# Node terms read in place by the matmuls of a graph kernel, instead of through ScalarE's copies

## The chip, the cores and the metric

The kernel runs on one core of a Trainium2 chip. The engines of the core are named as the profile names them: PE is TensorE, the matrix engine (PEld is its loading of weights), DVE is VectorE, ACT is ScalarE, POOL is GpSimd and SP is SyncE, which only starts transfers. PEq, ACTq and so on are the sequencers of the engines: they step through registers, waits and branches and hand the work to the engine behind them.

The metric is the time on the device for one execution, in microseconds (us). Before the change it was 9471.33 us, the median of three runs (9468.83 to 9475.12).

## The reference

The input is a graph: 6250 nodes with 256 features and 200000 edges, sorted by the node they go to (`dst`). Three things are computed: three graph attention layers over the edges, a linear attention over all nodes, and a layer of eight experts with two per node. The change lies in the graph attention, which reads, cut to what matters:

```
def _gat_conv(h, src, dst, W, att_src, att_dst, bias, heads, concat):
    xh = (h @ W).reshape(n, heads, d)
    a_s = (xh * att_src).sum(-1)
    a_d = (xh * att_dst).sum(-1)
    alpha = jax.nn.leaky_relu(a_s[src] + a_d[dst], NEG_SLOPE)
    amax = jax.ops.segment_max(alpha, dst, num_segments=n)
    e = jnp.exp(alpha - amax[dst])
    z = jax.ops.segment_sum(e, dst, num_segments=n)
    alpha = e / (z[dst] + 1e-16)
    out = jax.ops.segment_sum(xh[src] * alpha[:, :, None], dst, num_segments=n)
    ...
for i, (W, a_s, a_d, b, g, be, heads, concat) in enumerate(layers):
    h_new = _layernorm(_gat_conv(h, src, dst, W, a_s, a_d, b, heads, concat), g, be)
    if i > 0:
        h_new = h_new + h
    h = jax.nn.relu(h_new)
```

The term that matters is `a_d[dst]`, four numbers for each node that must reach each of its edges.

## The kernel before

**Tiling.** The nodes lie in 49 blocks of 128. The edges, sorted by `dst`, are cut into slots of 128 edges; two slots make a group, and all edges of a group go to nodes of one block. Ten groups make a window (20 slots), and a layer has 83 windows, so there are 249 windows in all. The function `edge_phase` works through the windows of one layer. Buffers that end in a number are rings of four windows (`RING`).

**What a window needs.** POOL gathers the rows of the source nodes, one indirect transfer for each slot (L1123, 20 of them, into `G`), and may run four windows ahead of the sums that read them. PE spreads the node term `a_d` over the edges of a slot: a matmul (`spread_ad`, L1275, 20 of them, 128x12 in bf16) multiplies the 0/1 matrix `OHT` with the block's term, which is kept as three bf16 parts for each of the four heads (`terms`, 12 numbers for a node, written by DVE once a layer before the edges begin). DVE makes the scores from it (L1455 to L1467), PE turns them (`turn`, L1284), DVE scans them for the greatest of each node (L1476 onward), PE turns that back (`turn_back`, L1292), DVE subtracts (L1543), ACT takes the exponentials (L1150, L1151). DVE weighs the gathered rows (L1563) and makes the one-hot matrices (L1555), PE sums the edges of each group into PSUM (`sums`, L1317), and DVE adds that to `acc`, the accumulator of the node block (L1581). When a node's edges go on in the next window, the old greatest value is replaced: PE spreads the factor (`spread_fade`, L1304), ACT takes its exponential (`fades`, L1160), and DVE's next scan waits for it.

**Order.** Each engine has its own order written out. A step of PE in window w is: sums of groups 0 to 4, `spread_fade(w+1)`, `turn(w+2)`, sums of groups 5 to 8, `spread_ad(w+3)`, the sum of group 9, matmuls of the linear attention that are mixed in, `turn_back(w+2)`. A step of ACT is: `make_index` (w+5), `exponentials(w+1)`, `load_node(w+4)`, `fades(w+1)`, mixed-in work. At the start of a layer ACT does `make_index` four times and `load_node` four times before its first exponential.

**Which block.** The block of each group depends on the data. A number for each window (`words`) holds the block of group 0 in its lowest six bits and then one bit for each further group that says whether the block moves on by one. `blocks_of` (L1014 to L1023) loads this word into a register of the engine that asks (an instruction TENSOR_LOAD) and works the ten block numbers out in registers. Before the change ACT and DVE ask for it: DVE to know which part of `acc` it adds to, ACT for `load_node` (L1137 to L1143), which copies the 128x12 terms of the ten blocks into a `node` buffer, from which PE's matmuls read at fixed addresses. `load_node` waits until the matmuls of the window four earlier are done (`ad_spread`), and PE waits for `load_node` (`node_ready`).

Of the kernel before, what the change touches and what calls it, by code (L numbers as in the profile page):

```python
# [21 lines left out]
P = 128  # L22
# [12 lines left out]
WG = 10  # L35
# [776 lines left out]
def edge_phase(nc, layer, st, io, dr):  # L812
# [13 lines left out]
    with Phase(nc, f"edges{layer}") as ph:  # L826
        G = [ph.sb(f"G{r}", [P, WS, GW]) for r in range(RING)]
        index = [ph.sb(f"index{r}", [P, WS], I32) for r in range(RING)]
        node = [ph.sb(f"node{r}", [P, WG, KEPT], BF16) for r in range(RING)]
        masks = ph.sb("masks", [P, RING, 1 + 3 * P], BF16)  # L830
# [41 lines left out]
        rels_in = ph.sem("rels_in")  # L872
        node_ready = ph.sem("node_ready")
        front_ready = ph.sem("front_ready")
# [254 lines left out]
        def _(a):  # L1129
# [6 lines left out]

            def load_node(i, n):  # L1137
                w = RING * i + n

                wait_past(a, ad_spread, w - RING + 1)  # L1140
                for g, b in enumerate(blocks_of(a, w)):
                    ins = a.activation(node[n][:, g, :], terms[:, bass.ds(b, 1), :, :].rearrange("p a h k -> p (a h k)"), ACT.Copy)  # L1142
                ins.then_inc(node_ready, 1)  # L1143

            def exponentials(i, n):
# [16 lines left out]
            for n in range(RING):  # L1162
                make_index(0, n)
            for n in range(RING):
                load_node(0, n)

            def step(i, n, mix):
                if mix:
                    centres(i, n)
                if exists(i, n, 1 + RING):  # L1170
                    make_index(*later(i, n, 1 + RING))
                if exists(i, n, 1):
                    exponentials(*later(i, n, 1))
                if exists(i, n) and exists(i, n, RING):
                    load_node(i + 1, n)
                if exists(i, n, 1):
                    fades(*later(i, n, 1))
                if mix:
                    mixes(i, n)
# [86 lines left out]
        def _(pe):  # L1266
            def spread_ad(i, n):
                w = RING * i + n
                pe.wait_ge(oht_ready, 2 * w + 2)
                pe.wait_ge(node_ready, w + 1)  # L1270

                wait_past(pe, ad_ready, w)
                wait_past(pe, ran, w)
                for s in range(WS):
                    mm = pe.matmul(ps_ad[:, s * KEPT:(s + 1) * KEPT], OHT[:, s, :], node[n][:, s // 2, :], start=True, stop=True)  # L1275
                mm.then_inc(ad_spread, 1)
# [1359 lines left out]
```

## Time and profile before

| what | value |
|---|---|
| median of three runs | 9471.33 us (9468.83 to 9475.12) |
| time of the profiled execution | 9454.66 us |
| its span | 9453.0 us |
| granted TensorE clock, mean over the span | 0.724 |
| PE busy | 5285.4 us (56%) |
| DVE busy | 5524.3 us (58%) |
| POOL busy | 5206.4 us (55%) |
| ACT busy | 1795.1 us (19%) |
| L1123, gathers of POOL | 4749.2 us, 4980 of them |
| L1317, sums of PE | 3620.3 us, 9960 matmuls |
| L1142, copies of ACT | 495.9 us, 2490 of them |
| L1275, matmuls that spread the node terms | 173.3 us, 4980 of them |

The profile is of one execution. No engine is busy for more than 58% of the span, so the time is made of waits between engines more than of work. A line of a timeline gives the start, the busy time, the engine, the line of the kernel, what it writes and reads, how many alike follow each other, and in brackets the idle time of the engine before it with what ended that wait. "issue" there means that the profile shows nothing that the engine waited for, and "remote" that a semaphore of another engine ended the wait and no single instruction could be named. Line numbers are those of the kernel before; the change takes 10 lines out ahead of the exponentials and 13 ahead of PE's matmuls.

### The profile page before, as it was taken

The page shows a single profiled execution, that of the slowest core. Times are in us where ns is not written, and L with a number is a line of the kernel's source. Part 1 is how long each engine was busy: PE and PEld are TensorE (multiplying, and loading weights), DVE is VectorE, ACT ScalarE, POOL GpSimd, SP SyncE. Part 2 cuts the span into 40 slices and gives each one's busy share as a digit, 9 for nine tenths or more (in the row PEclk, how much of TensorE's full clock was granted, in tenths as well). Part 3 has the DMA queues.
Part 4 walks back from the last instruction along what each step waited for, and adds up shares of the span by engine and source line. Part 5 has one row for each costly group of instructions (what it writes and reads, how often), then busy time and mean ns, then how long its engine had stood idle before and what let it go on. Part 6 is the DMA issues. An engine that isn't in the chain of part 4 may idle for free. (4 is left out here: it accounts for less than half of the span.)

```text
span 9453.0 us, 126480 instructions
## 1 busy us (share of the span) xinstructions
PE 5285.4 (56%) x21872; PEld 3724.2 (39%) x21873; DVE 5524.3 (58%) x14694; ACT 1795.1 (19%) x6145; POOL 5206.4 (55%) x5539
## 2 busy tenths in 40 slices
PE   4256666655556255565655556266656565553397
PEld 2144444433334144444443334144444443333255
DVE  4355655555558366665665558366666665557543
ACT  2011111110103012222210002122222220102333
POOL 3566666666662565656566662566666666661332
PEclk7677777776667577777776676577777777766699
DMA  3444444444442343444343333344444443334333
GB/s 118 113 137 130 138 130 136 136 129 133 131 132 87 105 117 111 119 113 118 114 117 110 108 112 108 106 114 121 120 120 120 122 116 112 111 107 132 113 55 75
DMA packets 540784, 1098.15 MB, mean 116 GB/s; under 512 B 136232, under 2 KB 332639, under 8 KB 540147
## 3 DMA queue, kind: packets, MB, share of 16 engines
q0 software_dynamic: 274368, 731.65, 28.9%
q1 hardware_dynamic: 264803, 361.17, 12.1%
q14 instruction: 400, 3.28, 0.1%
q8 instruction: 61, 1.00, 0.0%
q10 hardware_dynamic: 1152, 1.05, 0.0%
HBM read 953.54 MB, written 148.64 MB: 117 GB/s over the span
## 5 line engine op out<-in xcount | busy, mean ns | idle before, releaser
L1123 POOL DMA_INDIRECT edges_G<-rows,edges_index x4980 | 4749.2, 954 | 3076.4 <-issue 1389.8
L1317 PE MATMUL edges_ps_o<-edges_G,edges_OH 128*128 128x264 f32 x9960 | 3620.3, 517 | 2818.6 <-DVE acc L1581 1740.4
L1317 PEld LDWEIGHTS edges_ps_o<-edges_G,edges_OH 128*128 128x128 f32 x9960 | 2357.1, 253 | 3772.9 <-DVE acc L1581 1852.1
L1581 DVE TENSOR_TENSOR acc<-acc,edges_ps_o 128x264 f32 x2490 | 1056.9, 424 | 1992.7 <-remote 1038.9
L1563 DVE TENSOR_TENSOR edges_G<-edges_G,edges_ps_c 128x1024 f32<-128x1024 f32 x1245 | 1501.5, 1206 | 44.1 <-ACT edges_G L1151 33.3
L1142 ACT ACTIVATE edges_node<-terms 128x12 bf16 x2490 | 495.9, 210 | 2316.7 <-issue 2283.7
L1555 DVE TENSOR_TENSOR edges_OH<-edges_ps_c,relT 128x512 f32<-128x512 f32 x1245 | 847.1, 681 | 30.5 <-issue 19.2
L1150 ACT ACTIVATE edges_ps_c<-edges_diff 128x80 f32<-128x80 f32 x249 | 60.0, 241 | 2402.8 <-DVE edges_diff L1543 2174.5
L2400 POOL DMA_INDIRECT x<-experts_Y,experts_token x105 | 162.1, 1544 | 373.5 <-issue 211.5
L1476 DVE TENSOR_TENSOR_SCAN edges_run<-edges_masks,edges_ps_s 128x128 f32<-128x128 bf16 x249 | 102.9, 413 | 444.0 <-ACT edges_fade L1160 286.9
L1275 PEld LDWEIGHTS edges_ps_s<-edges_node,edges_OHT 128*128 128x128 bf16 x4980 | 181.5, 104 | 296.6 <-issue 248.8
L1275 PE MATMUL edges_ps_s<-edges_node,edges_OHT 128*128 128x12 bf16 x4980 | 173.3, 172 | 219.9 <-issue 123.7
L1449 DVE TENSOR_SCALAR edges_OHT<-edges_rels,lane 128x1280 bf16<-128x1280 bf16 x498 | 258.8, 561 | 0.0
L2423 PE MATMUL experts_psH<-W,experts_xs 128*128 x420 | 209.6, 622 | 43.5 <-issue 43.3
L1543 DVE TENSOR_TENSOR edges_diff<-edges_alpha,edges_ps_s 128x80 f32<-128x80 f32 x249 | 57.2, 230 | 301.4 <-DMA xn<-node_Hn 106.3
L799 PE MATMUL node_psB<-node_Wx,node_hT 128*128 128x264 f32 x588 | 213.8, 500 | 0.0
L1988 POOL DMA_INDIRECT xslot<-final_XH,final_slots x98 | 97.6, 996 | 198.0 <-DVE final_slots L2168 169.9
L2438 PE MATMUL experts_psY<-W,experts_hT 128*128 x840 | 198.8, 379 | 0.9 <-DVE experts_hT L2527 0.9
L583 POOL DMA_DIRECT2D rows<-node_ext x147 | 80.0, 544 | 212.1 <-ACT node_ext L757 172.3
L2520 DVE TENSOR_TENSOR experts_hid<-experts_psH,b 128x512 f32<-128x512 f32 x105 | 72.6, 691 | 210.9 <-PE experts_psH L2423 202.9
L1444 DVE TENSOR_SCALAR edges_front<-edges_ps_c,edges_rels 128x128 f32<-128x128 f32 x249 | 85.3, 343 | 133.2 <-DMA edges_rels<-rel 60.1
L1304 PEld LDWEIGHTS edges_ps_s<-edges_dropped,edges_front 128*128 128x128 f32 x498 | 119.7, 241 | 108.8 <-issue 80.7
(345 smaller groups left out, 6399.7 us busy)
## 6 DMA issues: line engine op xcount, KB each, us to landing
edges_rels<-rel SPq DMA_DIRECT2D x249, 640.0 KB
edges_G<-rows,edges_index POOLq DMA_INDIRECT x4980
xslot<-edges_blank SPq DMA_DIRECT2D x80, 650.0 KB
edges_links<-links SPq DMA_DIRECT2D x1992, 0.1 KB
rows<-node_ext POOLq DMA_DIRECT2D x147, 130.0 KB, 2.4
edges_masks<-lanes SPq DMA_DIRECT2D x996, 15.0 KB
experts_X<-xslot SPq DMA_DIRECT2D x105, 130.0 KB, 2.1
node_rows<-rows SPq DMA_DIRECT2D x98, 130.0 KB, 2.1
```

The lines of the kernel that those rows point to most:

```text
L799: pe.matmul(psB[slot % 2][:, 0:RW + H], hT[:, slot % TILE_RING, k, :], Wx[:, k, :], start=(k == 0), stop=False)
L1123: g.indirect_dma_start(G[n][:, s, 0:RW], None, dr["rows"], bass.IndirectOffsetOnAxis(index[n][:, s:s + 1], 0)).then_inc(gathered[n], 16)
L1142: ins = a.activation(node[n][:, g, :], terms[:, bass.ds(b, 1), :, :].rearrange("p a h k -> p (a h k)"), ACT.Copy)
L1275: mm = pe.matmul(ps_ad[:, s * KEPT:(s + 1) * KEPT], OHT[:, s, :], node[n][:, s // 2, :], start=True, stop=True)
L1317: mm = pe.matmul(ps_o[BANK_OF[g]][:, 0:GW], OH[:, 2 * g + j, :], G[n][:, 2 * g + j, :], start=(j == 0), stop=(j == 1))
L1449: v.tensor_scalar(OHT[:, s, :].rearrange("p s e -> p (s e)"), rels[:, c * WG * P:(c + 1) * WG * P], lane[:, 0:1], None, ALU.is_equal).then ...
L1555: v.tensor_tensor(OH[:, 4 * k:4 * k + 4, :], ps_iota.unsqueeze(1).broadcast_to([P, 4, P]), rel.unsqueeze(2).broadcast_to([P, 4, P]), ALU.i ...
L1563: v.tensor_tensor(g4[:, :, :, 0:D], g4[:, :, :, 0:D], ps_w[:, 4 * k:4 * k + 4, :].unsqueeze(3).broadcast_to([P, 4, H, D]), ALU.mult).then_ ...
L1581: v.tensor_tensor(a, a, ps_o[BANK_OF[g]][:, 0:GW], ALU.add).then_inc(added, 1)
L2400: g.indirect_dma_start(dr["x2"], bass.IndirectOffsetOnAxis(token[:, slot, :], 0), Y[:, slot, :], None, compute_op=ALU.add).then_inc(y_out, 16)
L2423: mm = pe.matmul(psH[slot % 2][:, :], xs[:, slot % 2, k, :], W1[:, bass.ds(e, 1), k, :].rearrange("p a f -> p (a f)"), start=(k == 0), sto ...
L2438: mm = pe.matmul(psY[slot % 2][:, 0:C], hT[:, slot % 2, c * P:(c + 1) * P], W2[:, bass.ds(e, 1), c, :].rearrange("p a o -> p (a o)"), star ...
```

## The change

ACT's `load_node`, its four `node` buffers and the semaphore `node_ready` are gone. `spread_ad` on PE works out the block numbers of the window itself with `blocks_of` and gives the matmul a slice of `terms` whose address comes out of a register. Nothing is computed otherwise. The functions of DVE, POOL and SP are as before.

```diff
--- before.py
+++ after.py
@@ -826,7 +826,6 @@
     with Phase(nc, f"edges{layer}") as ph:
         G = [ph.sb(f"G{r}", [P, WS, GW]) for r in range(RING)]
         index = [ph.sb(f"index{r}", [P, WS], I32) for r in range(RING)]
-        node = [ph.sb(f"node{r}", [P, WG, KEPT], BF16) for r in range(RING)]
         masks = ph.sb("masks", [P, RING, 1 + 3 * P], BF16)
         links = ph.sb("links", [P, RING, 2, WS], BF16)
         rels = ph.sb("rels", [P, WS * P], BF16)
@@ -870,7 +869,6 @@
         gathered = [ph.sem(f"gathered{r}") for r in range(RING)]
         masks_in = [ph.sem(f"masks_in{r}") for r in range(RING)]
         rels_in = ph.sem("rels_in")
-        node_ready = ph.sem("node_ready")
         front_ready = ph.sem("front_ready")
         oht_ready = ph.sem("oht_ready")
         oh_ready = ph.sem("oh_ready")
@@ -1134,14 +1132,6 @@
                 a.activation(index[n][:, :], srcT[:, bass.ds(w * WG, WG), :].rearrange("p g j -> p (g j)"), ACT.Copy
                              ).then_inc(index_ready, 1)
 
-            def load_node(i, n):
-                w = RING * i + n
-
-                wait_past(a, ad_spread, w - RING + 1)
-                for g, b in enumerate(blocks_of(a, w)):
-                    ins = a.activation(node[n][:, g, :], terms[:, bass.ds(b, 1), :, :].rearrange("p a h k -> p (a h k)"), ACT.Copy)
-                ins.then_inc(node_ready, 1)
-
             def exponentials(i, n):
                 w = RING * i + n
                 a.wait_ge(diff_ready, w + 1)
@@ -1161,8 +1151,6 @@
 
             for n in range(RING):
                 make_index(0, n)
-            for n in range(RING):
-                load_node(0, n)
 
             def step(i, n, mix):
                 if mix:
@@ -1171,8 +1159,6 @@
                     make_index(*later(i, n, 1 + RING))
                 if exists(i, n, 1):
                     exponentials(*later(i, n, 1))
-                if exists(i, n) and exists(i, n, RING):
-                    load_node(i + 1, n)
                 if exists(i, n, 1):
                     fades(*later(i, n, 1))
                 if mix:
@@ -1266,13 +1252,14 @@
         def _(pe):
             def spread_ad(i, n):
                 w = RING * i + n
+                blocks = list(blocks_of(pe, w))
                 pe.wait_ge(oht_ready, 2 * w + 2)
-                pe.wait_ge(node_ready, w + 1)
 
                 wait_past(pe, ad_ready, w)
                 wait_past(pe, ran, w)
                 for s in range(WS):
-                    mm = pe.matmul(ps_ad[:, s * KEPT:(s + 1) * KEPT], OHT[:, s, :], node[n][:, s // 2, :], start=True, stop=True)
+                    at = terms[:, bass.ds(blocks[s // 2], 1), :, :].rearrange("p a h k -> p (a h k)")
+                    mm = pe.matmul(ps_ad[:, s * KEPT:(s + 1) * KEPT], OHT[:, s, :], at, start=True, stop=True)
                 mm.then_inc(ad_spread, 1)
 
             def turn(i, n):
```

How PE's order changes is seen in the loop of layer 0, between the last matmuls of group 8 and those of group 9. Before (`edges_ps_s` is the PSUM tile that takes the spread terms, ISA and REGISTER_ALU are steps of the sequencer, L809 and L1312 are waits with a computed count):

```order
L1312 REGISTER_ALU
L809 REGISTER_ALU
L1317 MATMUL edges_ps_o<-edges_G,edges_OH 128x264 x2
L1269 ISA
L1270 REGISTER_ALU
L1275 MATMUL edges_ps_s<-edges_node,edges_OHT 128x12 x20
L809 REGISTER_ALU
L1317 MATMUL edges_ps_o<-edges_G,edges_OH 128x264 x2
```

After, on the same engine at the same place (L1014 is `blocks_of`, L1262 the matmul of before's L1275, L1304 the sums):

```order
L1299 REGISTER_ALU
L809 REGISTER_ALU
L1304 MATMUL edges_ps_o<-edges_G,edges_OH 128x264 x2
L1014 ISA
L1014 TENSOR_LOAD words
L1014 ISA x2
L1256 ISA
L1262 REGISTER_ALU
L1262 ISA
L1262 MATMUL edges_ps_s<-terms,edges_OHT 128x12 x2
L1262 REGISTER_ALU x2
L1262 ISA
```

Ten pairs of matmuls stand there with two REGISTER_ALU and an ISA between each two pairs, and then the same two rows of group 9 as before; the one run of 20 matmuls has become ten pairs behind a load from memory into a register. On ACT, at the same time in the program, this is where the exponentials lead into `load_node` before:

```order
L1150 ACTIVATE edges_ps_c<-edges_diff 128x4x20
L1151 ACTIVATE edges_G<-edges_diff 128x4x20
L1016 TENSOR_LOAD words
L1016 ISA x2
L1142 REGISTER_ALU
L1142 ISA
L1142 ACTIVATE edges_node<-terms 128x12
L1142 REGISTER_ALU x2
L1142 ISA
```

The copies go on to ten, and then comes L1160, the exponential of the fade. After, from `make_index` to the first mixed-in work:

```order
L1132 ACTIVATE edges_index<-srcT 128x20
L1140 ACTIVATE edges_ps_c<-edges_diff 128x4x20
L1141 ACTIVATE edges_G<-edges_diff 128x4x20
L1150 ACTIVATE edges_fade<-edges_ps_s 128x4
L1172 ACTIVATE edges_xs<-edges_ps_r 128x256
```

L1150 is now the exponential of the fade; it follows the two exponentials of the scores at once. ACT's step has lost ten copies and the register steps of its sequencer that led to them (on average 19 ALU_OP, 10 FUSED_REGOPS and one TENSOR_LOAD a window).

## Rows read from the trace of the kernel before

**Rows 1.** The page, busy time, share of the span and instructions of an engine.
```profile
PE 5285.4 (56%) x21872; PEld 3724.2 (39%) x21873; DVE 5524.3 (58%) x14694; ACT 1795.1 (19%) x6145; POOL 5206.4 (55%) x5539
```

**Rows 2.** The page, costliest groups: count, busy, mean ns of one, idle before.
```profile
L1123 POOL DMA_INDIRECT edges_G<-rows,edges_index x4980 | 4749.2, 954 | 3076.4 <-issue 1389.8
```

**Rows 3.** Waits of POOL, ACT, PE, DVE: total us, times, longest.
```profile
POOL edges_G L1123 <- remote: 1212.5, 369, 5.7
...
ACT edges_node L1142 <- issue: 2283.7, 1159, 7.2
...
PE edges_ps_o L1317 <- DVE acc L1581: 1740.4, 586, 13.9
...
DVE acc L1581 <- remote: 1038.9, 296, 9.0
...
DVE edges_run L1476 <- ACT edges_fade L1160: 286.9, 47, 12.1
...
DVE edges_run L1476 <- issue: 99.9, 35, 6.6
```

**Rows 4.** Timeline around 2202 us: start, busy, engine, line, idle before.
```profile
2202.23 0.17 ACT L1160 ACTIVATE edges_fade<-edges_ps_s 128x4 f32<-128x4 f32 x1 [1.89 <-issue]
...
2202.50 0.42 DVE L1476 TENSOR_TENSOR_SCAN edges_run<-edges_masks,edges_ps_s 128x128 f32<-128x128 bf16 x1 [7.25 <-ACT edges_fade L1160]
...
2203.08 0.94 POOL L1123 DMA_INDIRECT edges_G<-rows,edges_index  x1 [3.10 <-remote]
```

**Rows 5.** Timeline, start of layer 0.
```profile
320.43 0.48 PE L1292 MATMUL edges_ps_s<-ident,edges_greatest 128*128 128x128 f32 x1 [1.85 <-issue]
...
350.82 0.24 DVE L1543 TENSOR_TENSOR edges_diff<-edges_alpha,edges_ps_s 128x80 f32<-128x80 f32 x1 [29.99 <-DMA xn<-node_Hn]
...
351.12 0.94 POOL L1123 DMA_INDIRECT edges_G<-rows,edges_index  x1 [0.30 <-issue]
...
366.28 0.21 ACT L1142 ACTIVATE edges_node<-terms 128x12 bf16 x1 [3.34 <-issue]
...
368.52 1.22 DVE L1563 TENSOR_TENSOR edges_G<-edges_G,edges_ps_c 128x1024 f32<-128x1024 f32 x1 [16.38 <-ACT edges_G L1151]
...
382.88 0.94 POOL L1123 DMA_INDIRECT edges_G<-rows,edges_index  x1 [30.82 <-PE edges_ps_o L1317]
```

**Rows 6.** Timeline, start of layer 1.
```profile
3177.72 0.24 DVE L1543 TENSOR_TENSOR edges_diff<-edges_alpha,edges_ps_s 128x80 f32<-128x80 f32 x1 [29.87 <-DMA h<-node_Hn]
...
3195.97 1.22 DVE L1563 TENSOR_TENSOR edges_G<-edges_G,edges_ps_c 128x1024 f32<-128x1024 f32 x1 [16.93 <-ACT edges_G L1151]
...
3210.34 1.01 POOL L1123 DMA_INDIRECT edges_G<-rows,edges_index  x1 [29.96 <-PE edges_ps_o L1317]
```

**Rows 7.** Timeline, start of layer 2.
```profile
6047.28 0.21 ACT L1142 ACTIVATE edges_node<-terms 128x12 bf16 x1 [3.98 <-issue]
...
6055.17 0.24 DVE L1543 TENSOR_TENSOR edges_diff<-edges_alpha,edges_ps_s 128x80 f32<-128x80 f32 x1 [17.47 <-DMA h<-node_Hn]
...
6056.40 1.21 DVE L1563 TENSOR_TENSOR edges_G<-edges_G,edges_ps_c 128x1024 f32<-128x1024 f32 x1
...
6070.73 1.04 POOL L1123 DMA_INDIRECT edges_G<-rows,edges_index  x1 [33.22 <-PE edges_ps_o L1317]
```

**Rows 8.** Sequencer steps by line: count, ns min/median/max, first and last start.
```profile
L1142 ACTq ALU_OP  x4731: 2/38/1683, 252.3 to 8512.4; - x198
...
L1312 PEldq ALU_OP  x768: 32/32/36, 625.1 to 8542.7; - x192
...
L2371 PEldq FUSED_REGOPS  x330: 42/151/168, 8915.1 to 9419.8; - x165
...
L2371 PEldq TENSOR_LOAD <-owner x210: 296/303/632, 8914.5 to 9419.2; - x105
```

**Rows 9.** Timeline, the 20 matmuls of one window at 2017 us.
```profile
2017.81 0.71 PE L1275 MATMUL edges_ps_s<-edges_node,edges_OHT 128*128 128x12 bf16 x20
```

**Rows 10.** Window at the end of layer 0: length, busy PE, PEld, DVE, ACT, POOL.
```profile
2858.00:2875.00 17.00, 12.54 (x46) 8.59 (x44) 15.59 (x38) 0.68 (x3) 0.00 (x0) 0.90 0.00 0
```

## The prediction

> **What bounds the kernel now.** I read the page first: no engine is busy for more than 58% of the span [rows 1], so what counts is who waits for whom. The group of POOL's gathers comes next: 4980 of 0.954 us each with 3076.4 us of idle time before them [rows 2]. The ordinary gap between two gathers is 0.30 us [rows 5], so one costs 0.954 + 0.30 = 1.25 us, a window of 20 costs 25 us, and all 249 windows 6245 us. Of the idle time 4980 x 0.30 = 1494 us is that gap; 1582 us is more than it. Three waits take 30.82 + 29.96 + 33.22 = 94 us of that, one at the start of each layer, where POOL has filled its four windows and waits for the first sums [rows 5 to 7]. The other 1488 us are 6.0 us a window. So a window takes 25 + 6 = 31 us, and POOL's gathers are four fifths of it. A change gains only if it makes those 6 us smaller, or the three waits of 30 us.
>
> Then the waits of each engine, to see what the 6 us are. POOL waited 1212.5 us in 369 waits, 3.3 us each, for sums; PE waited 1740.4 us for DVE's additions; DVE waited 1038.9 us for PE's results [rows 3]. They wait for each other in a ring. A timeline shows how: PE finished turning back a window at 320.43 + 0.48 us, and DVE, which wants just that, started at 350.82, with POOL gathering without a break until 352 [rows 5]. PE's result was 30 us old when DVE saw it. At the end of layer 0, where POOL gathers nothing, DVE is busy 15.59 of 17 us [rows 10]: there the same ring has hardly a wait. So results of PE reach the others late while something else is going on, and gathers are the first suspect. ACT's copies are the second. Their sequencer steps take 38 ns at the median but up to 1683 [rows 8], and the idle time before the copies is 2283.7 us in 1159 waits that nothing in the profile ended [rows 3]: ACT crawls through register steps through much of the span.
>
> **Part by part: ACT at the starts of the layers.** ACT has 40 copies to make before its first exponential. In layer 0 the last of them is at 366.28; the scores were there at 350.82, and DVE waited 16.38 us for the exponential, until 368.52 [rows 5]. Layer 2 shows the same pair with ACT free, from 6055.17 to 6056.40, 1.23 us apart [rows 7]. With no copies, layer 0 gains 368.52 - 350.82 - 1.23 = 16.5 us, and layer 1 3195.97 - 3177.72 - 1.23 = 17.0 us [rows 6]. In layer 2 the copies ended at 6047.28, before the scores, so ACT's order cost nothing; but DVE's wait of 17.47 us ended only 8 us after them, with POOL still since 6070.73 - 33.22 = 6037.5: between 0 and 17.5 us. Sure are 33.5 us, and with half of layer 2 it is 42. The upper bound is all of POOL's three waits, 94 us, if PE's results also come through earlier without ACT's crawl beside them. Between 42 and 94 I take the middle, 68 us. All of it counts in the span, since POOL stands still and the whole layer is shifted. What is late next there is PE's held result, then the 14 us of DVE and PE from the exponential to the first free buffer.
>
> **ACT in the windows.** `load_node` stands ahead of `fades`, and DVE's scan waits for the fade. DVE lost 286.9 us in 47 waits that ended with the fade, and 99.9 us in 35 more before the same scan [rows 3]: 387 us in all, the upper bound for this term; the lower is 0, since a wait for the fade only may cover one that comes anyway. One such place: fade at 2202.23, scan at 2202.50 after 7.25 us, POOL's gather at 2203.08 after 3.10 us [rows 4]. A pause of POOL of that length is no more than its mean, 3.3 us, so what the fade costs the span is at most POOL's pause and not DVE's 7.25. For the 47 waits that is 47 x 3.3 = 155 us. The pause would often be there for another late result, so I take half, 78 us. What is late next is PE's result for DVE's addition, as in the 296 waits for it. The 495.9 us of the copies themselves count nothing beyond this: ACT is the idlest engine. The wait of ACT on `ad_spread` and that of PE on `node_ready` go too; PE's matmuls of window w+3 had `node` filled a window before, so nothing was waiting there but at the layers' starts.
>
> **PE.** Each window adds, ahead of and between the 20 matmuls, the steps that ACT had: 4731 / 249 = 19 ALU_OP [rows 8], ten FUSED_REGOPS and one TENSOR_LOAD. On PE's sequencer an ALU_OP takes 32 ns, a FUSED_REGOPS 151 and a TENSOR_LOAD 303 [rows 8], from the experts' code for the last two: 0.61 + 1.51 + 0.30 = 2.42 us. The 20 matmuls took 0.71 us in a run [rows 9] and would lie inside it, so the step is longer by 1.7 us where nothing hides it. Behind it on PE stand the sum of group 9, the mixed-in matmuls and `turn_back`, and DVE and POOL wait for all three. Bounds: 249 x 1.7 = 426 us lost, and 0. That the block is read in `terms` and not in `node` costs nothing: same partitions, same 12 numbers, address given a register earlier.
>
> The Trainium skill bears on this twice. It says (Advanced Engine Details and Errata, Engine Queue Depths) that TensorE's queue is 64 deep and the others' 8: by that the chain would be hidden whenever 2.4 us of matmuls are queued, and the term nearer 0; no row here shows the depth. And it says (Runtime: NRT & Kernel Launch, Instruction fetch mechanics) that loading a register costs about 200 ns; the row has 303, and by the page the chain would be 0.1 us a window shorter.
>
> **The sum.** -68 - 78 + 50 = -96 us on the profiled execution's own 9454.66 us: 9359 us. That execution is 16.7 us below the median of the runs, so the median to expect is 9471.33 - 96 = 9375 us.
>
> **Rivals.**
> Layer starts only. The gathers' pace takes up what the fades give, because the pause of POOL is ended by a late PE result and not by the fade. For it: 369 waits of POOL against 47 of DVE for the fade. Then the time is 9471 - 68 + 50 = 9453, or 9403 with PE's chain hidden; about 9428.
>
> PE's chain is on the path. The wait ahead of group 8 ends late in most windows, the queued work is short, and group 9 and `turn_back` come 1.7 us later in each. It decides from (68 + 78) / 249 = 0.59 us exposed a window. Fully exposed it costs 426 us, the fades then gain nothing, as PE is the late one, and the layer starts 68: 9471 + 426 - 68 = 9829. At half of it, 0.85 us or 212 us, it is 9615. For it: DVE's 296 waits for PE's results, 3.5 us each. Against: PE is busy for 56% of the span, and its results are held up for microseconds after they are done, which hides a delay of one or two.
>
> ACT's crawl is what holds PE's results. Then the pauses of POOL shrink everywhere. If half of the 6 us a window goes, it is 249 x 3 = 747 us, about 8720. If a quarter goes it is 373 us, 9098. For it: DVE's wait in layer 2 went on for 17.7 us after POOL's last gather had ended, with ACT crawling through ten of them [rows 7]. Against: in the windows the waits end in POOL's pauses, and a gather costs 1.25 us whatever ACT does.
>
> The change doesn't do what it says for the time: crawl and copies were only a sign of POOL's transfers and covered by them, the 33 us at the starts come back as later waits for the held results, and PE's chain costs the rest: 9471 within 19 us.
>
> **How the numbers follow.** The forecast has a chance of 0.34, layer starts only 0.22, of which 0.17 beyond what can be measured, the large gain 0.12: 0.63 for faster. No difference is the other 0.05 and 0.12 for the change that does nothing: 0.17. PE's chain has 0.20. Faster means by over 0.2%, 19 us, about what a measurement of this kernel can tell from no change. The likeliest case's own range is 9280 to 9440 us, from the fades' 155 and the starts' 94 to a smaller gain of each. The range for 8 in 10 runs from 9120, which takes in the fades' 387 us and reaches nearly to a quarter of the large gain, to 9600, where PE's chain is half exposed.
>
> **What would show it.** In the profile after: L1142 gone and DVE's first weighing within 2 us of the scores' difference in all three layers, against 17 now; POOL's three waits below 20 us each instead of 30; DVE's waits for the fade under 100 us. The 20 matmuls of a window spread over less than 2.5 us, with the wait of the additions for PE not longer than now. The forecast is wrong if the three waits of POOL stay near 30 us, if a window still takes 31 us with DVE's waits merely renamed, or if the sum of group 9 follows group 8 by over 2 us in most windows while POOL waits for it.

## The result, and the profile after

The changed kernel takes 9729.69 us (median of four runs, 9694.83 to 9751.17), the kernel before beside it 9473.10 us. The ratio is 1.0268, with a 95% interval of 1.0237 to 1.0299: 257 us slower, where 96 us faster was forecast and 9600 us was the upper end of the range. The profiled execution took 9723.87 us with a span of 9722.2 us. In the fences of the changed kernel, before's L1123 (gathers) is L1121, L1160 (fade) L1150, L1275 (matmuls that spread the node terms) L1262, L1292 (`turn_back`) L1279, L1317 (sums) L1304, L1476 (DVE's scan) L1463, L1543 (difference of the scores) L1530, L1563 (weighing) L1550 and L1581 (addition) L1568; the further runs move some lines again. A register step that takes over 0.3 us is called slow below, and "crawl" is the state in which many steps are slow.

The page of the changed kernel: POOL's busy time and its gathers answer to [rows 1, 2], and beside them stand the matmuls that spread the node terms.

```profile
PE 5283.8 (54%) x21872; PEld 3771.9 (39%) x21873; DVE 5516.7 (57%) x14694; ACT 1314.8 (14%) x3654; POOL 5218.6 (54%) x5539
...
L1121 POOL DMA_INDIRECT edges_G<-rows,edges_index x4980 | 4759.8, 956 | 3337.4 <-issue 1393.5
...
L1262 PE MATMUL edges_ps_s<-terms,edges_OHT 128*128 x4980 | 475.0, 177 | 1989.8 <-issue 1813.0
```

POOL's idle time before the gathers was 3076.4 us [rows 2] and is 3337.4: 261 us more, and the span is 9722.2 - 9453.0 = 269 us longer. Nearly all of the loss is waiting of POOL. The idle time of PE before the 20 matmuls is 1989.8 / 249 = 8.0 us a window.

The waits of the changed kernel, which answer to [rows 3]:

```profile
POOL edges_G L1121 <- PE edges_ps_o L1304: 1172.4, 401, 31.1
POOL edges_G L1121 <- remote: 736.5, 245, 5.4
...
PE edges_ps_s L1262 <- issue: 1813.0, 889, 63.1
PE edges_ps_o L1304 <- DVE acc L1568: 1088.8, 432, 12.1
...
DVE acc L1568 <- remote: 918.7, 253, 9.6
DVE acc L1568 <- PE edges_ps_o L1304: 582.4, 178, 11.9
...
DVE edges_diff L1530 <- PE edges_ps_s L1279: 110.9, 54, 4.7
...
DVE edges_run L1463 <- ACT edges_fade L1150: 78.8, 15, 9.8
```

Two lines of the kernel before stand in no group of rows and belong beside these:

```profile
POOL edges_G L1123 <- PE edges_ps_o L1317: 439.2, 229, 33.2
...
DVE acc L1581 <- PE edges_ps_o L1317: 120.9, 74, 5.1
```

POOL's waits for sums ("remote" and PE together) were 1212.5 + 439.2 = 1651.7 us and are 736.5 + 1172.4 = 1908.9: 257 us more, of the 269 that the span is longer. PE waits less for DVE's additions than before (1088.8 against 1740.4 us), since it now spends that time, and more, ahead of L1262 on "issue". DVE waits for the fade for 78.8 us instead of 286.9, as was forecast, but its wait for PE's sums has grown from 120.9 to 582.4 us. The sequencer steps say what "issue" is (count, ns min/median/max); they answer to [rows 8]:

```profile
L1262 PEldq ALU_OP  x4731: 2/36/1702, 255.3 to 8818.2; - x198
L1262 PEldq FUSED_REGOPS  x2490: 3/53/1606, 255.4 to 8818.3; - x192
...
L1014 PEldq TENSOR_LOAD <-words x249: 296/302/829, 250.8 to 8814.3; - x125
```

The median of an ALU_OP is 36 ns, but the greatest is 1702: what ACT's steps did before, PE's do now. Over all ALU_OP and FUSED_REGOPS of the two traces, 1850 of ACT's 9625 steps were slow before and none of PE's 5068; in the changed kernel none of ACT's 1840 and 1291 of PE's 12682. The slow steps have moved with the chain. The matmuls of one window in the timeline; they answer to [rows 9], which are of another window:

```profile
2215.58 0.15 PEld L1262 LDWEIGHTS edges_ps_s<-terms,edges_OHT 128*128 128x128 bf16 x1
2216.01 1.14 PE L1262 MATMUL edges_ps_s<-terms,edges_OHT 128*128 x12
...
2217.37 0.20 PE L1262 MATMUL edges_ps_s<-terms,edges_OHT 128*128 x2 [0.21 <-issue]
...
2219.01 0.20 PE L1262 MATMUL edges_ps_s<-terms,edges_OHT 128*128 x2 [1.44 <-issue]
...
2220.56 0.54 PE L1262 MATMUL edges_ps_s<-terms,edges_OHT 128*128 x4 [1.36 <-issue]
2220.72 0.43 DVE L1568 TENSOR_TENSOR acc<-acc,edges_ps_o 128x264 f32 x1 [3.58 <-remote]
...
2221.20 2.12 PE L1304 MATMUL edges_ps_o<-edges_G,edges_OH 128*128 128x264 f32 x4
2221.22 1.01 POOL L1121 DMA_INDIRECT edges_G<-rows,edges_index  x1 [2.39 <-remote]
```

The first 12 matmuls follow each other in 1.14 us; then a pair comes only every 1.4 to 1.6 us, and the last four end at 2221.1. What was 0.71 us is 5.5 us from the first weight load on, and the sum of group 9 (2221.20) stands behind it. Over all windows the sum of group 9 starts 8.6 us after that of group 8 has ended, against 1.9 before, and over 2 us after it in 97% of the windows, against 27%: the prediction's own sign of a wrong forecast. DVE's addition and POOL's gather in this fence don't wait for that sum, which ends only at 2223.3: the addition is of group 8, whose sum had ended at 2216.2, 4.5 us earlier. Both kinds of wait are there. In the 144 windows in which POOL stands idle for over 0.8 us ahead of the gathers that need the sum of group 9, it goes on 1.5 us after that sum's end (before: 204 windows, 6.7 us), so there the late sum itself is what it waits for; for the sums of groups 5 and 7 it goes on 8 to 10 us after their end, in both kernels. The start of layer 0, which answers to [rows 5]:

```profile
345.81 0.24 DVE L1530 TENSOR_TENSOR edges_diff<-edges_alpha,edges_ps_s 128x80 f32<-128x80 f32 x1 [31.27 <-DMA xn<-node_Hn]
...
347.04 1.22 DVE L1550 TENSOR_TENSOR edges_G<-edges_G,edges_ps_c 128x1024 f32<-128x1024 f32 x1
...
356.40 1.23 PE L1262 MATMUL edges_ps_s<-terms,edges_OHT 128*128 x8 [8.75 <-issue]
...
359.25 0.20 PE L1262 MATMUL edges_ps_s<-terms,edges_OHT 128*128 x2 [1.61 <-issue]
...
363.26 0.20 PE L1262 MATMUL edges_ps_s<-terms,edges_OHT 128*128 x2 [3.81 <-issue]
...
367.90 0.20 PE L1262 MATMUL edges_ps_s<-terms,edges_OHT 128*128 x2 [4.45 <-issue]
...
369.69 0.87 PE L1262 MATMUL edges_ps_s<-terms,edges_OHT 128*128 x6 [1.59 <-issue]
...
370.47 0.45 PE L1279 MATMUL edges_ps_s<-ident,edges_greatest 128*128 128x128 f32 x1
...
374.92 0.95 POOL L1121 DMA_INDIRECT edges_G<-rows,edges_index  x1 [23.87 <-PE edges_ps_o L1304]
```

DVE weighs 1.23 us after the scores' difference, not 17.7: its wait for ACT is gone. But the ten blocks of the fourth window on PE now take from 356.40 to 370.56, with `turn_back` and the first sums behind them, and POOL's wait is 23.87 us instead of 30.82. The three waits of POOL are 23.9, 24.4 and 31.2 us, 79.4 together against 94.0: 14.6 us are gained there instead of 68.

### The profile page after: what moved, and what is told of

It reads as the page before. It is cut to its first block and busy times, and to the rows that moved or that the text cites. A ratio compares the mean times of both kernels' runs of the same rounds, so it can differ in the third digit from the quotient of the medians.

```text
span 9722.2 us, 123665 instructions
## 1 busy us (share of the span) xinstructions
PE 5283.8 (54%) x21872; PEld 3771.9 (39%) x21873; DVE 5516.7 (57%) x14694; ACT 1314.8 (14%) x3654; POOL 5218.6 (54%) x5539
## 5 line engine op out<-in xcount | busy, mean ns | idle before, releaser
L1121 POOL DMA_INDIRECT edges_G<-rows,edges_index x4980 | 4759.8, 956 | 3337.4 <-issue 1393.5
L1304 PE MATMUL edges_ps_o<-edges_G,edges_OH 128*128 128x264 f32 x9960 | 3287.1, 481 | 1776.1 <-DVE acc L1568 1088.8
L1304 PEld LDWEIGHTS edges_ps_o<-edges_G,edges_OH 128*128 128x128 f32 x9960 | 2206.3, 236 | 2528.5 <-DVE acc L1568 1168.4
L1568 DVE TENSOR_TENSOR acc<-acc,edges_ps_o 128x264 f32 x2490 | 1055.1, 424 | 2221.2 <-remote 918.7
L1262 PE MATMUL edges_ps_s<-terms,edges_OHT 128*128 x4980 | 475.0, 177 | 1989.8 <-issue 1813.0
L1550 DVE TENSOR_TENSOR edges_G<-edges_G,edges_ps_c 128x1024 f32<-128x1024 f32 x1245 | 1501.5, 1206 | 5.3 <-issue 5.3
L1262 PEld LDWEIGHTS edges_ps_s<-terms,edges_OHT 128*128 128x128 bf16 x4980 | 312.5, 106 | 2234.4 <-issue 2217.5
L1530 DVE TENSOR_TENSOR edges_diff<-edges_alpha,edges_ps_s 128x80 f32<-128x80 f32 x249 | 58.2, 234 | 657.9 <-DMA h<-node_Hn 332.8
L1150 ACT ACTIVATE edges_fade<-edges_ps_s 128x4 f32<-128x4 f32 x249 | 43.2, 174 | 1973.1 <-PE edges_ps_s L1271 662.2
L1463 DVE TENSOR_TENSOR_SCAN edges_run<-edges_masks,edges_ps_s 128x128 f32<-128x128 bf16 x249 | 102.1, 410 | 159.2 <-ACT edges_fade L1150 78.8
L1558 DVE TENSOR_TENSOR acc<-acc,edges_fade 128x260 f32 x249 | 107.3, 431 | 120.5 <-issue 104.6
```

The costliest lines, as they stand in the source:

```text
L1121: g.indirect_dma_start(G[n][:, s, 0:RW], None, dr["rows"], bass.IndirectOffsetOnAxis(index[n][:, s:s + 1], 0)).then_inc(gathered[n], 16)
L1304: mm = pe.matmul(ps_o[BANK_OF[g]][:, 0:GW], OH[:, 2 * g + j, :], G[n][:, 2 * g + j, :], start=(j == 0), stop=(j == 1))
L1550: v.tensor_tensor(g4[:, :, :, 0:D], g4[:, :, :, 0:D], ps_w[:, 4 * k:4 * k + 4, :].unsqueeze(3).broadcast_to([P, 4, H, D]), ALU.mult).then_ ...
L1568: v.tensor_tensor(a, a, ps_o[BANK_OF[g]][:, 0:GW], ALU.add).then_inc(added, 1)
```

## The experiments

Chips differ in this case, so each ratio is to the kernel before on the same chip, and the time of that kernel is given with it. Profiles of before are those of the first chip, at 9454.66 us; against them only differences of many per cent of a wait are read. Eighteen further runs were made.

**The chain of steps, or the copies, or the place of reading.** Kernel before 9462.32 us.

e1, PE reads a fixed block:

```diff
-                blocks = list(blocks_of(pe, w))
-                    at = terms[:, bass.ds(blocks[s // 2], 1), :, :]
+                    at = terms[:, 0:1, :, :]
```

> The kernel after, but every matmul that spreads node terms reads block 0 at a fixed address, so neither PE nor ACT works out block numbers in registers; left out is the right block, all else is done. Theory A (PE's register steps crawl beside POOL's gathers and stand ahead of the last sums): well below the kernel before, 9473 less the 68 to 150 us that ACT's copies cost, so 9320 to 9410 us, and PE's idle time before the 20 matmuls falls from 8.0 us a window to under 2. Rival B (what costs is that ACT's copies no longer separate the engines, or that the matmuls read `terms` itself): stays near 9730 us.

Measured: 9409.69 us, ratio 0.9942 (0.9925 to 0.9959), at the upper edge of what theory A expected (L1261 is the spreading matmul here). From the page:

```profile
L1121 POOL DMA_INDIRECT edges_G<-rows,edges_index x4980 | 4760.6, 956 | 3017.1 <-issue 1390.7
...
L1261 PE MATMUL edges_ps_s<-terms,edges_OHT 128*128 128x12 bf16 x4980 | 170.9, 172 | 180.7 <-issue 139.3
```

The idle time before the 20 matmuls is 0.7 us a window. So PE's steps cost the way from 0.9942 to 1.0268, 0.0326 x 9473 = some 310 us (the two intervals together leave 275 to 345). What `load_node` on ACT had cost is 53 us, if reading `terms` in place costs nothing, and nothing speaks against that: a matmul takes 172 ns on average in both kernels. POOL's three waits at the layers' starts are 18.6, 20.2 and 31.1 us here, 24 us less than before: with no chain on ACT or PE at all, the starts give 24 us and not 68.

e2, the changed kernel with `load_node` put back on ACT, its copies unread:

> The kernel after, with ACT's ten copies a window and their register steps put back beside PE's; nobody reads the copies. Theory A, with ACT's chain on the path too, at the starts and before the fades: 9730 plus 70 to 150 us, 9800 to 9880. Rival C (ACT's chain never cost anything, or the engines' crawl is shared, so that two chains make each other slower): 9730 within 20 us if it cost nothing, over 9950 if they slow each other.

Measured: 9841.25 us, ratio 1.0401 (1.0381 to 1.0422), 1.3% or some 125 us above the changed kernel's ratio: within theory A's range. DVE's wait for the fade is back:

```profile
DVE edges_run L1475 <- ACT edges_fade L1158: 257.9, 39, 10.5
```

e3, the kernel before with ACT's copies at fixed addresses:

```diff
-                for g, b in enumerate(blocks_of(a, w)):
-                    ins = a.activation(node[n][:, g, :], terms[:, bass.ds(b, 1), :, :]...
+                for g in range(WG):
+                    ins = a.activation(node[n][:, g, :], terms[:, g:g + 1, :, :]...
```

> The kernel before, but ACT's ten copies read blocks 0 to 9 at fixed addresses: the copies stay, their register steps go; left out are the right blocks. Theory A says that the steps and not the copies cost: 9473 less 70 to 150 us, 9320 to 9400, within 20 us of the kernel with fixed blocks on PE. Rival D (the copies themselves matter, or nothing on ACT does): 9473 within 20 us.

Measured: 9430.97 us, ratio 0.9963 (0.9951 to 0.9976), a gain of 31 us: less than the 70 to 150 of theory A and more than rival D's 20. The copies then stand without a gap:

```profile
L1142 ACT ACTIVATE edges_node<-terms 128x12 bf16<-128x12 bf16 x2490 | 278.4, 198 | 0.0
```

So ACT idled ahead of its copies on their register steps alone, 2316.7 us before and 0.0 here, and those steps were worth 0.4% of the time.

e4, `spread_ad` behind the sum of group 9 instead of ahead of it:

> The kernel after, with the matmuls that spread the node terms moved behind the sum of group 9 on PE; nothing is left out. If what costs is that the last sum of the window (and with it the buffers that POOL waits for, and DVE's last addition) stands behind the crawling steps, the time falls by a third to all of the loss, to 9480 to 9650 us. If it is the results behind them (scores of window w+3, and turn_back), or only the total of PE's sequencer time, it stays at 9730 within 30 us.

Measured: 9889.79 us, ratio 1.0469 (1.0435 to 1.0503). Slower still by 2.0%, which neither expectation had: it is not the sum of group 9 alone that waits. `turn_back` now stands right behind the chain, and DVE's difference of the scores wants its result:

```profile
L1530 DVE TENSOR_TENSOR edges_diff<-edges_alpha,edges_ps_s 128x80 f32<-128x80 f32 x249 | 59.0, 237 | 1445.5 <-PE edges_ps_s L1279 893.1
...
DVE edges_diff L1530 <- PE edges_ps_s L1279: 893.1, 130, 16.5
```

DVE's idle time there is 1445.5 us, from 657.9 in the changed kernel and 301.4 in the kernel before; 893.1 us of it are put down to `turn_back`, from 110.9 in the changed kernel (in its waits above). What stands behind the chain on PE pays for it.

**How long the chain is, and where.** Kernel before 9371.38 us, another chip.

e5, one block number for all 20 matmuls:

```diff
-                blocks = list(blocks_of(pe, w))
+                blocks = [next(blocks_of(pe, w))] * WG
```

> The kernel after, but all 20 matmuls of a window read the block of group 0: one load into a register and one mask instead of ten numbers; left out are the right blocks of groups 1 to 9. Theory A says that what costs is the number of register steps between the matmuls (29 of them, some at 0.7 us beside POOL's gathers): with 3 of them left, close to the kernel with fixed blocks, 9410 to 9450 us. Rival E (the load from memory into a register, or a matmul with an address out of a register, costs most of the 320 us): 9600 or more.

Measured: 9320.40 us, ratio 0.9945 (0.9928 to 0.9961), the same as with no register at all (0.9942). The load into a register and the address out of one cost nothing that is measured here.

e6, five numbers, each for two groups:

```diff
+                blocks = [b for b, _ in zip(blocks_of(pe, w), range(5)) for _ in range(2)]
```

> The kernel after with five block numbers instead of ten, each read by two groups; left out are the right blocks. Theory A, cost in proportion to the steps: 9410 + 320 x 14/29 = 9565 us, between 9520 and 9620. Rival E: above 9680. A third (only a chain long enough to outlast the queued sums costs): below 9480.

Measured: 9341.45 us, ratio 0.9964 (0.9950 to 0.9978). Half the chain costs 0.2%, not the 1.6% of proportion. The time lies where the third theory put it (its 9480 stood for a kernel before of 9462, a ratio of 1.002), but its reason, a chain that outlasts the queued sums, isn't shown by this run: in a chain of 14 steps few are stretched at all, as the table shows.

```profile
L1262 PE MATMUL edges_ps_s<-terms,edges_OHT 128*128 x4980 | 253.4, 173 | 252.1 <-issue 105.6
```

1.0 us of idle time a window, against 8.0 for ten blocks. The table has, of each four steps of a chain, the share that is slow (over 0.3 us), over the 249 windows; the steps are ALU_OP and FUSED_REGOPS at the line of the copies or of the matmuls, 29 a window:

```
share of slow steps       1-4   5-8   9-12  13-16  17-20  21-24  25-28   first to last, mean
before, on ACT            0.02  0.05  0.17  0.31   0.38   0.44   0.34    12.3 us
after, on PE              0.00  0.00  0.08  0.39   0.39   0.25   0.12     9.8 us
e6, on PE (14 steps)      0.00  0.00  0.05  0.25                          2.3 us
e13, on PE, faster chip   0.00  0.00  0.00  0.00   0.00   0.00   0.00     3.2 us
```

(The 29th step, slow in 29, 10 and 0% of the windows, is left out.) A chain on PE starts fast every time and turns slow at about its twelfth step. The place of the step in the chain is one part of it, and how long POOL has gathered is another. Counting a run of gathers as broken by a gap of over 1 us, a step of ACT's chain in the kernel before was slow in 1% of the cases in the first 2 us of a run, in 29% at 5 to 6 us, and in 82 to 83% from 10 to 20 us. In the changed kernel, at 10 to 20 us of a run, none of 636 steps with places 1 to 8 was slow and 229 of 255 with places 17 to 29 were; in the first 2 us of a run, 18 of 258 of the latter.

e7, the chain woven between the sums, four blocks ahead of the sum of group 7, three ahead of 8, three ahead of 9:

> The kernel after with PE's 20 matmuls and their register steps woven between the sums: four blocks ahead of the sum of group 7, three ahead of group 8's, three ahead of group 9's. Nothing is left out. If the place of the chain makes the loss (it stands in one piece where nothing covers it), part of its steps now lies in PE's waits for DVE's additions and the time falls by 50 to 150 us, to 9580 to 9680. If the sequencer's total time makes the loss, it stays at 9730 within 30 us.

Measured: 9417.33 us, ratio 1.0052 (1.0035 to 1.0068). Nothing is left out, and four fifths of the loss are gone: 2.2% or some 200 us, where 50 to 150 were expected.

e8, the kernel before with added pauses in POOL's gathers:

```diff
+                    if k:
+                        for _ in range(2):
+                            g.value_load(words[0:1, 0:1], min_val=0, max_val=64 * 2 ** (WG - 1) - 1)
```

> The kernel before with four added pauses of about 1 us in each window of POOL's gathers (two register loads ahead of chunks 1 to 4, results unused); nothing is left out. Theory F: long unbroken runs of gathers are what slows register steps and holds PE's results; with shorter runs the crawl before ACT's copies falls clearly below 2284 us, and of the 4 us added a window much comes back out of POOL's own 6 us of waits, so less than 400 us are lost, 9470 to 9850. Rival: length of the runs doesn't matter; POOL's pauses add up, 249 x 4 = 1000 us, 10450 us, and the crawl is as before.

Measured: 9743.87 us, ratio 1.0393 (1.0375 to 1.0410), 368 us lost, within theory F's bound; ACT's idle time before its copies was 1757.1 us, against 2316.7 in the kernel before of the first chip. But the pauses weren't what they were meant to be:

```profile
2205.55 0.95 POOL L1126 DMA_INDIRECT edges_G<-rows,edges_index  x1 [0.30 <-issue]
2206.80 0.95 POOL L1126 DMA_INDIRECT edges_G<-rows,edges_index  x1 [0.30 <-issue]
2211.64 0.94 POOL L1126 DMA_INDIRECT edges_G<-rows,edges_index  x1 [3.89 <-issue]
```

Of the chunks with loads ahead of them, 54% still follow at 0.30 us, and others come after a longer gap, like the 3.89 us here. The runs of gathers didn't get shorter: by the count above there are 499 of 12.3 us on average, against 508 of 12.1 in the kernel before. So the run doesn't test theory F, though its time lies in that theory's range.

**A chip without the crawl.** Four runs were made on a chip on which the kernel before takes 7853.95 us, and the next four on another with 7852.45 us.

e9, the woven kernel in pieces of 2, 3, 3 and 2 blocks, ahead of groups 6 to 9:

> The kernel after with PE's chain woven in four pieces of 2, 3, 3 and 2 blocks ahead of the sums of groups 6, 7, 8 and 9; nothing is left out. The woven kernel with pieces of 4, 3 and 3 stood at a ratio of 1.005 to the kernel before. If only the first 11 or so steps of a burst are fast (its slow steps began at the twelfth), shorter pieces leave fewer slow ones: ratio 0.995 to 1.003. If the count of steps within some tens of microseconds matters and not the piece, or the earlier piece makes PE wait for DVE's scan: 1.003 to 1.012.

e10, ACT's copies in pieces of three, three and four around the fade and the mixed-in work:

> The kernel before with ACT's ten copies in three pieces: three ahead of the fade, three behind it, four behind the mixed-in work; the start of a layer is as before and nothing is left out. Part of the 53 us that ACT's chain costs by the kernels with fixed blocks comes back, that of the fades but not that of the starts: ratio 0.995 to 0.998. If the chain's cost lies in the starts alone: 1.000.

e11, `fades` ahead of `load_node` in ACT's step:

> The kernel before with the exponential of the fade ahead of all ten copies; nothing is left out. By the prediction's term for the fades 78 us would go, ratio 0.992; by the kernel with fixed copies (31 us in all, starts included) not more than 20 us, ratio 0.998. If the copies then come late for PE's matmuls: above 1.

e12, the fourth round of copies of a layer's start behind the first exponentials:

> The kernel before with the last of the four rounds of copies at the start of each layer moved behind the first exponentials and fade; nothing is left out. By the prediction's term DVE's 16 us of wait for the exponential goes in layers 0 and 1: 33 us less, ratio 0.9965, POOL's waits at the starts down from 31 to about 15 us in two layers. If PE's held results follow in its place: 1.000.

Measured: ratios 1.0002, 1.0000, 0.9997 and 0.9999, each within 0.001. They say nothing of the crawl, since there was none. From e11, the page and ACT's steps:

```profile
L1123 POOL DMA_INDIRECT edges_G<-rows,edges_index x4980 | 4728.1, 949 | 1550.9 <-issue 1484.3
...
L1142 ACTq ALU_OP  x4731: 5/38/43, 254.5 to 6930.9; - x198
```

POOL's idle time is 1550.9 us, that is the 0.30 us between gathers and some 60 us more, and no ALU_OP of the chain took over 43 ns. Without the crawl a window takes 25 us, and within a layer POOL's longest gap is 0.32 us, so it never waits for a sum: it gathers for 2081 us without a break, and still no step is slow. A long run of gathers alone doesn't make the crawl.

e13, the changed kernel unaltered:

> The kernel after, unchanged, beside the kernel before on one chip once more. If the chip shows the crawl (the kernel before takes 9370 to 9470 us), the ratio is 1.027 as before. If it does not (7854 us), POOL's gathers run without a wait, PE's chain of 3 to 4 us lies in PE's own waits and the ratio is 1.000 within 0.002; a rival says that the chain as such costs, 1.01 or more on any chip.

Measured: 7854.27 us, ratio 1.0000 (0.9990 to 1.0010). The change costs nothing on this chip, though the sum of group 9 follows that of group 8 by over 2 us in 97% of the windows here too (3.1 us on average):

```profile
L1121 POOL DMA_INDIRECT edges_G<-rows,edges_index x4980 | 4746.3, 953 | 1552.1 <-issue 1474.4
...
L1262 PEldq ALU_OP  x4731: 3/36/322, 255.7 to 6975.1; - x198
```

e14, the kernel before with e10's and e12's reorderings together:

> The kernel before with both of ACT's reorderings: its ten copies in pieces of three, three and four around the fade and the mixed-in work, and the fourth round of copies at a layer's start behind the first exponentials. Nothing is left out. On a chip with the crawl 0.993 to 0.997, as it reaches for the 0.994 of the kernels with fixed blocks; on one without it 1.000.

Measured: 0.9997 (0.9987 to 1.0006). e11 and e9 were repeated there as well (e15 and e16), at 0.9998 and 1.0003. The last two runs were made on a chip with the crawl, the kernel before at 9510.69 us. e17 is e14's kernel:

> The kernel before with both of ACT's reorderings, as in the run before of that kernel. On a chip with the crawl (the kernel before at 9370 us or more) 0.993 to 0.997, DVE's waits for the fade down from 287 us to under 150, and POOL's first two waits at a layer's start below 25 us; on a chip without it 1.000.

Measured: 9510.90 us, ratio 0.9998 (0.9989 to 1.0007). The forecast of 0.993 to 0.997 fell, although its signs came: DVE's wait for the fade (L1163 here) and POOL's first two waits, and ACT's idle time before the copies (L1144) with them.

```profile
L1144 ACT ACTIVATE edges_node<-terms 128x12 bf16 x2490 | 485.3, 209 | 1398.4 <-issue 1348.4
...
DVE edges_run L1487 <- ACT edges_fade L1163: 70.9, 13, 9.9
...
380.28 0.94 POOL L1123 DMA_INDIRECT edges_G<-rows,edges_index  x1 [22.58 <-PE edges_ps_o L1328]
```

ACT idles 1398.4 us instead of 2316.7, DVE waits 70.9 us for the fade instead of 286.9, POOL 22.6 and 22.0 us in the first two layers instead of 30.8 and 30.0, and the time does not move. Taking the wait for the fade away brings nothing, so another wait comes in its place.

e18 is e9's kernel:

> The kernel after with PE's chain in pieces of 2, 3, 3 and 2 blocks. On a chip with the crawl 0.995 to 1.003 if the first 11 steps of each piece are fast, 1.003 to 1.012 if the steps crawl wherever they stand, as with pieces of 4, 3 and 3 (1.005); on a chip without it 1.000.

Measured: 9559.79 us, ratio 1.0054 (1.0040 to 1.0068). Shorter pieces are no better than e7's: 41% of steps 13 to 16 are slow, and 842 of all 7221, against 903 in e7 and 1264 in the changed kernel. With two thirds of the slow steps still there, four fifths of the loss are gone; so what the weaving gains is mainly the place.

No version beat the kernel before with the right result.

## Why the prediction was wrong, point by point

**The step that failed** is the price of PE's chain: "On PE's sequencer an ALU_OP takes 32 ns, a FUSED_REGOPS 151 and a TENSOR_LOAD 303: 0.61 + 1.51 + 0.30 = 2.42 us", of which 0.2 us a window was taken. Measured is a chain of 9.8 us from its first step to its last, and 310 us or 1.2 us a window in the time (e1 against the result; e5 and e6 show that it is the number of steps). The prices came from rows where PE's steps don't crawl: 768 short waits in the loop, one or two at a time, and the experts' code, behind the last of the edges' gathers. The row that mattered stood beside them: the same 29 steps on ACT reached 1683 ns, and ACT idled 2283.7 us over them [rows 3, 8]. The prediction called this ACT's crawl and took it for a trait of ACT. It goes with the chain of steps, as the counts of slow steps on ACT and PE before and after show. The time comes out of two terms: 53 us gained by ACT's chain, where 146 were forecast, and 310 lost by PE's, where 50 were.

**The starts of the layers** (68 us) measured 14.6 us. The order part was right, 17.7 us became 1.23; but PE's chain of 14 us stands in front of the same `turn_back` and sums. That is the smaller part of the miss: without any chain (e1) the starts gain 24 us. The sure 33.5 us were not sure, since other waits take their place, and the upper bound of 94 rested on PE's results coming earlier without ACT's crawl, which they don't. The prediction named PE's held result as what would be late next, and gave it no price.

**The fades** (78 us) were worth nothing that can be measured: e17 takes three quarters of that wait away at 0.9998. The bound of 0 was right and the middle between the bounds was not. All that `load_node` on ACT cost is 53 us, by e1, against 146 forecast; where in the window these 53 us arise, beyond the 24 at the starts, no run shows.

**The rival that came nearest** is "PE's chain is on the path", chance 0.20, with 9615 at half and 9829 in full. Its place was right: the sum of group 9 follows the crawl, and in 144 windows POOL follows that sum. Its breaking point of 0.59 us a window was passed. That the measured 9730 lies between its two times is luck: they came from a chain of 2.4 us, exposed by half or in full, while the real one is four times as long, and 1.2 of its 9.8 us show in the time.

**"ACT's crawl is what holds PE's results"** is refuted by e1 and e3: with no such chain on ACT or PE a window still takes (4760.6 + 3017.1) / 249 = 31.2 us on such a chip. What holds these results isn't shown.

**The rule on the queue's depth** (the Trainium skill, Advanced Engine Details and Errata, Engine Queue Depths), by which the prediction had the chain hidden whenever 2.4 us of matmuls are queued, doesn't decide it. In the window above PE stands idle for 1.44 and 1.36 us between two pairs, with the next pair not yet given to it, so a crawling sequencer is not ahead of its engine. How deep the queue is, no run here shows.

**What stays open** is what the crawl is. On some chips it goes together with long runs of gathers and with a step's place in its chain; that the length of the run is a cause was not tested, since e8 didn't change it. Three chips of the further runs had it (9462, 9371 and 9510 us for the kernel before), two did not. Two plain differences of the chips can be put aside. The granted clock is no explanation: an ALU_OP of ACT's chain has a median of 38 ns on both kinds. Nor do POOL's transfers take longer: the packets of its queue filled 28.9% of 9453 us in the kernel before and 34.8% of 7852 us in e11, 2732 us in both. Whether it is traffic of POOL's descriptors, of instructions or of the semaphores wasn't tried.

## What to carry to other kernels

Price an instruction that moves to another engine by what it costs now, in its place and among its neighbours, and not by a row of the new engine from a quiet phase; if its steps are stretched for no reason that the profile shows, take the stretching along. Before moving work off an idle engine, ask what will stand behind it in order on the new one: here the steps behind 2317 us of idling on ACT cost 31 us (53 with the copies), and a like chain on PE, with less idling, 310. A short chain is nearly free: 14 steps a window cost 0.2%. If such a chain must run on the engine that others wait for, cut it up between waits that are there anyway: that alone brought 1.027 back to 1.005.

## What the runs showed of the hardware that was not expected

The same kernel took 7852 to 7854 us on two chips and 9371 to 9511 us on three, with the runs of that kernel on one chip within about 0.3% of each other. On those two no ALU_OP of ACT's chain exceeded 43 ns (e11) and POOL gathered without a wait; on the other three steps reached 1.7 us on ACT and on PE, and also on DVE (e1) and on POOL (e8). A change that is worth 1.000 on the one is 1.027 on the other. None of PE's 5068 steps was slow in the kernel before, where PE has no such chain in the windows, on a chip on which ACT's were slow 1850 times.
